# Attention's first loads issued inside the projection, and the probability scaling moved from VectorE to ScalarE

## The reference

```
mod = (silu(c) @ wmod).reshape(4, 6, 1, 512)          # shift, scale, gate, twice
h = layernorm(x) * (1 + ca) + sa
q = (h @ wq) -> 16 heads of 128 + 64 (rope);  c, k_pe = split(h @ wkv_a, 128 + 64)
k_nope, v = split(c @ wkv_b);  k = [k_nope, rope(k_pe)]
attn = softmax(causal(q k^T / sqrt(192)));  x = x + ga * ((attn v) @ wo)
h = layernorm(x) * (1 + cb) + sb
x = x + gb * (h + shared experts(h) + top-2 of 16 experts(h))
```

## Time and profile before

| | |
|---|---|
| median of 3 runs | 1533.46 us (1527.58 to 1537.03) |
| the profiled execution's own time | 1530.34 us |
| its span, first to last instruction | 1528.7 us |
| mean granted TensorE clock | 0.960 |
| PE busy / PEld busy | 1372.6 us (90%) / 1158.0 us (76%) |
| DVE busy / ACT busy / POOL busy | 941.5 us (62%) / 560.6 us (37%) / 395.7 us (26%) |
| PE's last product of the projection, first of attention | 256.9 us, 279.3 us |

### The profile page before, as it was taken

One profiled execution on the slowest core, in us unless ns is written; L12 is line 12 of the kernel. 1 busy time (PEld: TensorE's weight loads), 2 busy tenths in 40 slices (PEclk: granted clock), 3 DMA queues, 4 the chain that ended last, 5 costly groups with the idle time before them and its releaser, 6 DMA issues. The chain is left out here.

```text
span 1528.7 us, 23824 instructions
## 1 busy us (share of the span) xinstructions
PE 1372.6 (90%) x7108; PEld 1158.0 (76%) x7108; DVE 941.5 (62%) x1993; ACT 560.6 (37%) x1279; POOL 395.7 (26%) x314
## 2 busy tenths in 40 slices
PE   6848887599999998999989999998799899998994
PEld 3436775488888887888878888887687688787873
DVE  2456774377677778767796777875554343343438
ACT  2322222254445444444444544443321232232222
POOL 0002666200000318003090030820827000000035
PEclk9968999799999999999999999999899999999997
DMA  9976898799989756877679966682748778888357
GB/s 337 403 250 173 240 302 268 240 331 332 308 285 333 235 196 227 285 271 247 216 270 359 312 216 217 202 311 81 283 146 314 266 260 314 298 326 311 134 190 257
DMA packets 179955, 403.13 MB, mean 264 GB/s; under 512 B 24557, under 2 KB 81841, under 8 KB 169637
## 3 DMA queue, kind: packets, MB, share of 16 engines
q1 hardware_dynamic: 160968, 299.62, 58.1%
q0 software_dynamic: 18912, 102.57, 17.9%
HBM read 250.56 MB, written 151.57 MB: 263 GB/s over the span
## 5 line engine op out<-in xcount | busy, mean ns | idle before, releaser
L1067 ACT ACTIVATE a_pr<-a_pr,a_nmax 128x128 f32<-128x128 f32 (+3 forms) x256 | 142.2, 556 | 118.4 <-DVE a_nmax L1130 118.2
L1230 PE MATMUL a_psY<-a_pT,a_cv 128*128 128x256 f32 (+2 forms) x768 | 135.2, 326 | 1.9 <-DVE a_pT L1152 1.9
L1230 PEld LDWEIGHTS a_psY<-a_pT,a_cv 128*128 128x128 f32 x768 | 125.8, 190 | 14.6 <-issue 2.1
L1130 DVE CUSTOM_DVE_ANT_0 a_pr<-a_psS,a_mask 128x128 f32<-128x128 f32 (+3 forms) x256 | 115.3, 486 | 33.2 <-PE a_psS L1218 32.4
L102 PE MATMUL a_psX<-a_hT,a_wqk 128*128 128x512 f32 (+1 forms) x256 | 100.7, 393 | 22.0 <-DMA a_wqk<-wqk_d 22.0
L1138 DVE TENSOR_SCALAR a_pr<-a_pr,a_rinv 128x128 f32<-128x128 f32 (+3 forms) x256 | 113.6, 508 | 2.2
L1163 DVE TENSOR_TENSOR n_acc<-a_psZ,n_acc 128x512 f32<-128x512 f32 x125 | 86.2, 689 | 35.3 <-PE a_psZ L104 33.4
L1147 DVE TENSOR_TENSOR a_oT<-a_psY,a_oT 128x512 fp32r<-128x512 f32 x64 | 44.1, 689 | 96.8 <-ACT a_oT L1078 96.8
L104 PE MATMUL a_psX<-a_hT,a_wqk 128*128 128x512 f32 (+1 forms) x256 | 100.6, 393 | 0.0
L103 PE MATMUL a_psX<-a_hT,a_wqk 128*128 128x512 f32 (+1 forms) x256 | 100.5, 393 | 0.0
L102 PE MATMUL a_psZ<-a_mh,a_oT 128*128 128x512 f32 x250 | 98.2, 393 | 0.8 <-issue 0.8
(11 more groups left out here) (291 smaller groups left out, 3499.7 us busy)
## 6 DMA issues: line engine op xcount, KB each, us to landing
w1s_d<-a_ws SPq DMA_DIRECT2D x72, 512.0 KB, 2.9
a_wqk<-wqk_d SPq DMA_DIRECT2D x64, 512.0 KB, 4.9
a_mh<-mhl_d SPq DMA_DIRECT2D x32, 1024.0 KB, 6.5
s_ring<-w1s_d POOLq DMA_DIRECT2D x13, 2048.0 KB, 9.2
w2s_d<-a_ws SPq DMA_DIRECT2D x72, 256.0 KB, 3.4
qpe_d<-p_qs SPq DMA_DIRECT2D x64, 256.0 KB, 4.3
a_qpe<-qpe_d SPq DMA_DIRECT2D x64, 256.0 KB, 3.9
a_rw<-in_L_ffn_rw SPq DMA_DIRECT2D x128, 128.0 KB, 3.6
```

The source lines that it names most:

```text
L1067: nc.scalar.activation(pr[i], pr[i], ACT.Exp, bias=nmax[:, i:i + 1], scale=-1.0, accum_out=rsum[:, i:i + 1]).then_inc(ex, 1)
L1130: nc.vector.tensor_tensor_reduce(out=pr[i], in0=score[i][:, 0:w], in1=mask[:, S - w:S], scale=-1.0, scalar=3e38, op0=ALU.add, op1=ALU.min, ...
L1230: m = nc.tensor.matmul(psY[:, q0:S], cv[:, j, cs], pT[:, ps, o:o + w], start=n == 0, stop=n == 11)
```

## The change

Two edits go together. **At the border of projection and attention**, the tiles `a_wqk`, `a_qpe` and `a_rw` with their semaphores move to `Batch`, and SP issues their first ten loads (two query weights of 512 KB, two rotated queries of 256 KB, six raw pieces of 128 KB) in the projection, at the start of the last batch and ahead of its stores. The waits for the projection's stores leave the end of its block; they stand now in the attention block as `A.stored`, on SP ahead of the first `load_m`, on POOL ahead of `load(1)`, on ScalarE in head 1 ahead of its first `o_high`. For the space, one of the projection's two hT buffers is now attention's `a_hT` slot 1, and `a_oT` and `a_mh` lie at another address. **In attention**, the four scalings per head are ScalarE's, behind `split_high` and ahead of `q_high`.

```diff
@@ Batch @@
+        self.wqk = K.sb("a_wqk", [P, 2, 2, DC, P], F32R, ctx)
+        self.qpe = K.sb("a_qpe", [P, 2, S], F32R, ctx)
+        self.rw = K.sb("a_rw", [P, 2, 2 * F + D // 2], F32, ctx)
...
+    def stored(self, eng):
+        for u in range(2):
+            eng.wait_ge(self.out_h[u], 16 * (B // 2 + 1))
+            eng.wait_ge(self.out_q[u], 16 * (P // HALF) * (B * TB // 2 + 1))
+        eng.wait_ge(self.out_k, 32 * (B + 1))
+        eng.wait_ge(self.out_c, 16 * (B + 1))
@@ stage_project @@
-        hT = sb("p_hT", [P, 2, DC, 2, S], F32R)
+        hT = [sb("p_hT", [P, DC, 2, S], F32R), A.hT[:, 1]]
...
+                        else:
+                            sp.wait_ge(out_q[0], 32 * GH)
+                            for i in range(2):
+                                A.load_w(sp, i, i)
+                                A.load_q(sp, i, i)
+                                A.raw(sp, i, 0, i, False)
 
                         sp.wait_ge(h_hi, b * DC + DC)
...
                 run(sp, body)
-                for u in range(2):
-                    sp.wait_ge(out_h[u], 16 * (B // 2 + 1))
-                    sp.wait_ge(out_q[u], 16 * GH * (B * NG // 2 + 1))
-                sp.wait_ge(out_k, 32 * (B + 1))
-                sp.wait_ge(out_c, 16 * (B + 1))
@@ stage_attention, SP @@
-                for u in range(2):
-                    load_w(u, u)
-                    load_q(u, u)
-                raw(0, 0, 0, False)
-                raw(1, 0, 1, False)
+                A.stored(sp)
                 for v in range(2):
                     load_m(v, v)
@@ stage_attention, POOL @@
                 pool.wait_ge(pv, 3)
+                A.stored(pool)
                 load(1)
@@ stage_attention, ScalarE @@
+                def shares(g):
+                    act.wait_ge(rc, g + 1)
+                    for i in range(TB):
+                        nc.scalar.activation(pr[i], pr[i], ACT.Copy, scale=rinv[:, i:i + 1]).then_inc(nr, 1)
...
                         exps(g)
                         split_high(*todo[0])
+                        shares(g)
                         if not (last and u):
                             q_high(g + 1)
...
                         if u:
+                            if not early:
+                                A.stored(act)
                             o_high(g - 1, n, v * 2, early < 2)
@@ stage_attention, VectorE @@
                     nc.vector.reciprocal(rinv[:, :], rsum[:, :]).then_inc(rc, 1)
-                    dve.wait_ge(rc, g + 1)
-                    for i in range(TB):
-                        nc.vector.tensor_scalar(pr[i], pr[i], rinv[:, i:i + 1], None, ALU.mult).then_inc(nr, 1)
```

More of the change, by code:

```diff
@@ L157, in __init__, with load_w, load_q, raw @@
         self.cv = K.sb("a_cv", [P, TB, 2, P], F32R, ctx)
+        self.wqk = K.sb("a_wqk", [P, 2, 2, DC, P], F32R, ctx)
+        self.qpe = K.sb("a_qpe", [P, 2, S], F32R, ctx)
+        self.rw = K.sb("a_rw", [P, 2, 2 * F + D // 2], F32, ctx)
+        self.w_in, self.q_in = [K.sem("a_w_in0"), K.sem("a_w_in1")], [K.sem("a_q_in0"), K.sem("a_q_in1")]
+        self.raw_in = [K.sem("a_raw_in0"), K.sem("a_raw_in1")]
+        self.out_h, self.out_q = [K.sem("p_out_h0"), K.sem("p_out_h1")], [K.sem("p_out_q0"), K.sem("p_out_q1")]
+        self.out_k, self.out_c = K.sem("p_out_k"), K.sem("p_out_c")
+        self.K = K
+    def load_w(self, sp, g, u):
+        sp.dma_start(self.wqk[:, u].rearrange("p s c n -> p (s c n)").bitcast(F32),
+                     self.K.wqk_d[bass.ds(g % H, 1)].rearrange("a p s c n -> p (a s c n)")).then_inc(self.w_in[u], 16)
+    def load_q(self, sp, g, u):
+        sp.dma_start(self.qpe[:, u].bitcast(F32), self.K.qpe_d.rearrange("b h p n -> (b h) p n")[bass.ds(g, 1)]
+                     .rearrange("a p n -> p (a n)")).then_inc(self.q_in[u], 16)
+    def raw(self, sp, b, e, q, shared):
+        g_, w_, d_ = ("sg", "sw1", "sw2") if shared else ("rg", "rw1", "rw2")
+        one = bass.ds(e, 1)
+        row = slice(q * P, (q + 1) * P)
+        f_, o = slice(q // 2 * P, (q // 2 + 1) * P), q % 2 * (D // 2)
+        ins = self.K.ins
+        for n, src in enumerate((ins["L0_ffn_" + g_][one, row, :], ins["L0_ffn_" + w_][one, row, :],
+                                 ins["L0_ffn_" + d_][one, f_, o:o + D // 2])):
+            sp.dma_start(self.rw[:, b, n * F:(n + 1) * F], src.rearrange("a p f -> (a p) f")).then_inc(self.raw_in[b], 16)
+    def stored(self, eng):
[4 more added lines that the diff above has]
+        eng.wait_ge(self.out_c, 16 * (B + 1))
 def stage_weights(K, N, X, modcol):
@@ L673, in product @@
                 def product(out, u, w):
-                    return split3(nc, out, [(w(c, 0), w(c, 1), hT[:, u, c, 0], hT[:, u, c, 1]) for c in range(DC)])
+                    return split3(nc, out, [(w(c, 0), w(c, 1), hT[u][:, c, 0], hT[u][:, c, 1]) for c in range(DC)])
                 def body(j, last):
@@ L825, in stage_attention @@
         hT, cT, kpe, cv = A.hT, A.cT, A.kpe, A.cv
-        wqk = sb("a_wqk", [P, 2, 2, DC, P], F32R)
-        qpe = sb("a_qpe", [P, 2, S], F32R)
+        wqk, qpe, rw, w_in, q_in, raw_in = A.wqk, A.qpe, A.rw, A.w_in, A.q_in, A.raw_in
         qT = sb("a_qT", [P, 2, S], F32R)
@@ L840, in stage_attention @@
         rinv = sb("a_rinv", [P, TB], F32)
+        oT = sb("a_oT", [P, 4, 2, S], F32R)
+        mh = sb("a_mh", [P, 2, 2, 2, D], F32R)
+        acc = N.acc
         psS = K.ps("a_psS", [P, 3, 512], F32, ctx)
@@ L917, in _ @@
             def _(sp):
[L918 to L924, removed]
+                load_w = lambda g, u: A.load_w(sp, g, u)
+                load_q = lambda g, u: A.load_q(sp, g, u)
+                raw = lambda b, e, q, shared: A.raw(sp, b, e, q, shared)
                 def load_m(n, v):
@@ L928, in load_m @@
                                  K.mhl_d[bass.ds(n % PAIRS, 1)].rearrange("a p u s n -> (a p) (u s n)")).then_inc(mh_in[v], 16)
[L930 to L937, removed]
                 def keep(b, e, q):
```

17 lines of the change are left out of this document (5 added, 12 removed).

## The result

The change takes 1512.51 us (median; 1509.05 to 1518.97) against 1531.87 us of the kernel before beside it: a ratio of 0.9882, 95% interval 0.9857 to 0.9906. The forecast was 1511 us, with 1501 to 1525 as its range. The profiled execution took 1509.05 us with a span of 1507.4 us, against 1530.34 and 1528.7 before. First the page's row of busy times, and the group that is new on it.

A forecast was written before the change was run, and what follows sets the result against it. Attention was taken as bound by PE, whose transposes stall for the query's low part, with idleness at the border. From 1530.3 us, -20.6 (stalls and clock) + 2.7 + 1.6 - 2.6 = -18.9 gave 1511 us, range 1501 to 1525.

The forecast's parts named there:

- The nine stalls beside POOL: In nine attention heads beside POOL's SBUF work, PE's transposes wait for the query's low part; all go: -17.2 us.
- Rival 2: In attention POOL goes on holding VectorE, so half of the 20.6 us stays: 1522 us; chance 0.15.
- The scalings on ScalarE: Attention's four scalings per head take 2.0 us on ScalarE, hidden except in heads 0 to 2: +2.7 us.
- Rival 3: ScalarE becomes attention's bound, stalling each of 61 heads 1.1 us: 1578 us; chance 0.05.
- The clock: In attention two of the nine stalls are followed by granted clock drops; both go: -3.4 us.
- The late weight: In attention the scalings wait behind a late raw weight, so its 3.1 us stall grows: +1.6 us (-4.8 to +3.5).
- The border: Projection to attention: waits of 3.2 and 2.4 us go, loads ahead of stores delay 3.0 us: -2.6 us.
- Rival 1: At the border the early loads delay the last batch by 7.0 us instead of 3.0: 1515 us; chance 0.14.
- rival 4: The border does not move, as something other than the stores holds its end: 1514 us; chance 0.66 together with the forecast.

The follow-up runs named there:

- The two POOL experiments: POOL's addition of n_b done five times over: in the kernel before 1542.29 us, in the changed kernel 1510.27 us, both against 1530.52 us.
- The loads behind group 2: The change with its ten loads issued after the last batch's group 2 query stores; 1550.80 us against 1564.61 us of the kernel before, ratio 0.9898.
- the places alone: The kernel before with only its tiles allocated as in the change, loads, waits and scalings as before; 1534.87 against 1530.52 us, ratio 1.0022.
- the scalings alone: The kernel before with only the four scalings moved to ScalarE, no early load or moved tile; 1544.38 against 1564.61 us, ratio 0.9859.
- the border alone: The change with the scalings back on VectorE; 1565.77 us against 1564.61 us of the kernel before, ratio 1.0002.

## Why the prediction came out right

**The nine stalls beside POOL**: I took -17.2 us, and all nine are gone. The two POOL experiments show the cause: the same added work makes four more stalls and 9.5 us more of them beside POOL in the kernel before, and none in the changed one. Rival 2, that POOL goes on holding VectorE, fell as argued: the weight's low part runs beside ScalarE's scalings, and the query's low part ends 1.8 us before it is wanted, under POOL too. The lock of the Trainium skill (SBUF — State Buffer, SBUF: two separate sides) fits both: by that page ScalarE has a port of its own and never waits for the others. The trace agrees, as ScalarE's scalings take 1.91 us with POOL at rest and beside it.

**The scalings on ScalarE**: 1.91 us against my 2.0, hidden in the heads with slack. Rival 3, ScalarE as the bound, needed 3.8. The rule of the Trainium skill that VectorE is the faster engine where it has a performance mode (Perfetto Trace Analysis, Optimizing Scalar/DVE Operations) is true of the operation alone, 1.27 against 1.91 us, and decides nothing here, as the trace shows slack for 1.91 and none for 5.44. Heads 0 to 2 lost 2.80 - 2.05 + 0.88 + 0.89 = 2.5 us, for which I had 2.7.

**The clock** was the term sized worst. I counted the drops behind two of the nine stalls, 3.4 us. Attention's -18.3 us are the waits' -15.5, the addresses' +5.4 (60 heads of 0.09) and a remainder of -8.2. The four stretches at the low clock, with 1.7 us of PE's work each, give 6.8 of it; 1.4 us stay unexplained. A fifth stretch, behind head 63, makes up the -1.4 there. So the term was 3.4 and should have been about 8.4. Two of these stood behind stalls that I did not expect to vanish, in head 0 and at the late weight. There the drop went while the stall stayed, at 2.80 and 1.79 us, so a stall's length alone doesn't tell whether the clock falls.

**The late weight**: I took +1.6 us and it became 0.48 + 1.79 = 2.27 against 3.1, so -0.8. Its landing shifted: ScalarE's longest wait is 3.6 us, not 6.2. The step that failed took the wait of one trace as fixed, although head 44, which it held, now starts 13 us earlier and its transfers need not move with it. My lower bound had named that.

**The border**: I took -2.6 us and the first product came 1.0 us earlier. The mechanism was right, a copy that waits for a store behind the loads. The delay was mis-sized, 4.9 us (264.60 against 258.45 + 1.26 = 259.71, when POOL's part was ready) instead of 3.0. That is 5.6 - 4.9 = 0.7 us left, near the 1.0 measured. The loads behind group 2 confirm it by bringing the copy back on time. Rival 1, a delay of 7.0, wasn't reached.

**What the sum lacked**: the tiles' new places, +5.4 us. I had read the diff for instructions and waits, and taken moved tiles as costing nothing. Term by term the waits gave -15.5 us where I had -12.9 (-17.2 + 2.7 + 1.6), the clock -8.4 for -3.4, the border -1.0 for -2.6 and the places +5.4 for nothing: -19.5 of the 21.4 us in the traces. The clock missed by 5.0 and the places by 5.4, against each other. So the main cause was right, and that the total came within 2 us of the forecast is luck in part.

**The border edit as a whole** is worth nothing that could be measured (1.0002, 0.9975 to 1.0029): 1 us gained at the first product, and its own tile places take it back in attention, by 2.3 us in that kernel's trace and 6.2 in that of the places alone. At the first product rival 4, a border that does not move, was nearer in size (off by 1.0 us) than the forecast's own term (off by 1.6).

## What to carry to other kernels

If a short VectorE operation between SBUF tiles lies in a critical chain and grows several times whenever POOL works on SBUF, move it to ScalarE if its slower but steady duration fits into the slack, rather than shortening POOL's work. Before loads are put ahead of stores on one queue, ask which buffer those stores give back; and a wait for landing that is taken from the issuing engine may stand in the queue again. Compare the mean durations of unchanged matmuls before and after any edit that moves tiles: here one per cent of some of them cost more than the border edit gave.

## What was not expected of the hardware

- **Matmul time depends on where the operands lie.** L103's and L104's products of a_psX went from 389 to 394 and 395 ns, those of a_psZ from 389 and 390 to 393 and 394, with nothing but addresses changed; L102's stayed at 389 and 392. A gap of 976 bytes brought a_psX's to 390 and a_psZ's to 392.
- **Chips differ in one stage.** From the first feed-forward product to the end the kernel before took 452.1 us and the change 452.2 on one chip each; the scalings alone and the border alone took 485.5 and 485.6 on another. There PE's longest idle times in that stage, for which the profile shows no releaser ("issue"), are longer, first with the scalings alone, then with the change:

```profile
PE s_po L102 <- issue: 22.6, 3, 17.4
```
```profile
PE s_po L102 <- issue: 9.0, 3, 4.4
```

The granted clock of the stage is lower too, 0.93 against 0.96 (by the shortfall from 1.00 some 68 us at the low level instead of 36, so some 16 us of the 33). Which comes first, and what that chip does more slowly, wasn't studied.
- **The length of a stall doesn't tell whether the clock falls.** Head 0 had 1.00 with a stall of 2.80 us in the changed kernel, and 0.91 with 2.43 us in another and with 2.05 us in the kernel before.
